# Attention output kept transposed and divided by GpSimd, against transposed and divided per head on TensorE and VectorE

## The chip, the cores and the metric

One core of one Trainium2 chip runs the whole program. The metric is the device time of one execution in microseconds (us). TensorE (PE in the rows) multiplies matrices, VectorE (DVE) and ScalarE (ACT) work on its results, GpSimd (POOL) works in SBUF and issues its own transfers, and SyncE (SP) only issues transfers.

## The reference, cut to what matters

Four images of 32 x 32 tokens with 192 channels go through attention with 12 heads of 16 channels and a relative position bias, then through a feed-forward layer that sends each token to one of 8 experts.

```python
x = x + proj(attention(layernorm(x)))      # 4 images x 12 heads, n = 1024 tokens each
  # attn = softmax(q * scale @ k.T + bias)   (n x n);  out = attn @ v   (n x 16)
  # out of the 12 heads side by side, @ proj_w.T + proj_b
t = layernorm(x)
gate = t @ Wg.T + bg                        # the best of 8 experts for each token
out = t_x + p(expert) * W3 (silu(W1 t) * (W2 t))
```

The softmax is computed as exponentials of scores less a row maximum; the weighted values are divided by the sum of the exponentials at the end. This division is what the change moves.

## The kernel before, in words

**Stages.** `project` normalizes the tokens and makes queries, keys, values and the bias tables. `attention` runs over 48 steps, a head of an image each (image fastest: step n is head n // 4 of image n % 4). `gate` multiplies with the output projection, adds the residual, normalizes again and computes the gate. `route` sorts tokens by expert, `experts` computes them. Each stage is a block: all engines meet at its end.

**A step of attention.** Each engine follows a written order; steps 4 to 43 are a hardware loop of four on TensorE, ScalarE, VectorE and SyncE, while GpSimd's program is written out. TensorE goes through four rounds (u = 0 to 3). A round is two score tiles (L796, 128 keys x 512 queries each, in a ring of three PSUM banks), two raw score tiles (L762, 128 queries x 1024 keys, in two PSUM buffers) of a head one or two steps ahead, two score tiles more, and the weighted values (L808) of the round before. VectorE takes the maximum of each raw tile (L921): eight a head. ScalarE takes the exponential of each score tile (L904): sixteen a head. Raw tile t has to wait for the maximum of tile t - 2, since there are two buffers.

**The maxima's way.** When VectorE has a head's eight maxima (after round 0 of the step before it), GpSimd copies them (L658), TensorE transposes them at the end of round 1 (L787), ScalarE copies the result (L886) and SyncE stores it into the extra row of that head's query tile (L621).

**SyncE's order.** Step n: eight loads of products for head n + 3 (`load_products`, L526 to L530) once the scores of step n - 1 are through, the store of the maxima for n + 1, and eight loads of positions for n + 3 (`load_positions`, L541 and L542). TensorE waits for all sixteen of head n + 2 at round 1 of step n (L845).

**The output of a head, the part that is changed.** `out_ps` holds, for each quarter of the image's queries, 32 rows: 16 channels, the sum of the exponentials in row 16, zeros. ScalarE copies it to `out_t` after the fourth exponential of the next step (`copy_out`, L892). TensorE turns it at the end of round 2 (`turn_out`, L814: 16 weight loads and 16 small float32 passes into a bank of the score ring, position 13 of 18). VectorE inverts the sums and multiplies (`normalize`, L923: L931 and L936) into `att_sb`, token by token. The ring bank is free for scores again only when `att_done` has come (L779).

**GpSimd in attention.** Besides the values (L666) and the maxima's copies it splits the experts' weights: in steps 4 to 39 a load of 234 KB a step (L697, L701) and the split of one (L681 to L688), and every five steps a load (L713), a split (L720, L721) and a store (L722) of W3, 384 KB each.

**The start of `gate`.** SyncE loads W3 (L1250). For each half image s TensorE turns `att_sb` (`turn_attention`, L1081), ScalarE copies it (`copy_attention`, L1146), and TensorE projects (`project_out`, L1092); VectorE adds the residual and takes statistics (`residual`, L1200, L1204). GpSimd clears `slot_rows` (L1045) and normalizes (L1056).

## Time and profile before

| | us |
|---|---|
| median of 3 runs (lowest, highest) | 873.83 (872.3, 876.49) |
| the profiled execution, its own time | 873.62 |
| its span, first to last instruction | 871.6 |
| first to last start of L819 (`turn_out`) in the span | 155.8 to 640.8 |
| mean granted TensorE clock | 0.952 |

The profile is of one execution, and all positions are microseconds from the start of its span. A row of the timeline has a start, a length, the engine, the line, the operation and the tiles, a count where rows were merged, and in brackets the idle time before it with what ended it. PEld is TensorE's loading of weights, which runs beside its multiplying; a name with q at its end (SPq, POOLq) is the engine's queue issuing a transfer.

### The profile page before, as it was taken

The numbers are of one execution on the slowest core, as the hardware profiler recorded it, in microseconds if no ns is written. First come the engines' busy times: TensorE is split into PE (matmuls) and PEld (weight loads), VectorE is DVE, ScalarE is ACT, GpSimd is POOL, SyncE is SP. The second block draws the span as 40 slices with busy tenths as digits, with TensorE's granted clock in tenths as the row PEclk, the third lists the DMA queues.
The fourth block names the chain that finished last, engine by engine and source line by source line (L and its number), as shares of the span: only waits on it lengthen the run. The fifth ranks groups of instructions, "written<-read, shape, count | busy, mean of one in ns | idle before, by whom it ended". The sixth has DMA issues, their size and how long they took to land. (4 is left out here: it accounts for less than half of the span.)

```text
span 871.6 us, 32001 instructions
## 1 busy us (share of the span) xinstructions
PE 781.6 (90%) x11826; PEld 477.4 (55%) x11826; DVE 712.9 (82%) x983; ACT 628.8 (72%) x1142; POOL 288.7 (33%) x437
## 2 busy tenths in 40 slices
PE   4999939999999999999999999999989617999994
PEld 1678803444444444444444444444468516999994
DVE  5976768999999999998999999989537665888883
ACT  3676615888888888888888888888955514667662
POOL 5630000013343423302234233421114403677762
PEclk9999958999999999999999999999999757999998
DMA  6346963444554455445444555554044403555560
GB/s 178 81 132 188 366 227 106 107 121 139 141 145 140 133 129 137 118 119 143 111 139 134 139 143 135 150 140 111 4 164 131 166 25 74 121 138 122 137 108 13
DMA packets 89866, 114.56 MB, mean 131 GB/s; under 512 B 40267, under 2 KB 56809, under 8 KB 88274
## 3 DMA queue, kind: packets, MB, share of 16 engines
q1 hardware_dynamic: 79248, 80.35, 33.9%
q0 software_dynamic: 9248, 26.51, 11.4%
q10 hardware_dynamic: 1314, 6.95, 2.1%
q8 instruction: 36, 0.59, 0.3%
q14 instruction: 20, 0.16, 0.1%
HBM read 77.58 MB, written 33.19 MB: 127 GB/s over the span
## 5 line engine op out<-in xcount | busy, mean ns | idle before, releaser
L921 DVE TENSOR_REDUCE neg_max<-max_ps 128x1 f16<-128x1024 f32 x384 | 452.3, 1221 | 38.3 <-PE max_ps L762 30.4
L904 ACT ACTIVATE probs<-ring_ps 128x512 f32<-128x512 f32 x768 | 413.6, 596 | 67.1 <-PE ring_ps L796 58.1
L796 PE MATMUL ring_ps<-q_side,k_side 113*32 113x512 f16 x3072 | 239.0, 383 | 8.3 <-DMA q_side<-rel_split 4.8
L808 PE MATMUL out_ps<-probs,values 128*32 128x256 f32 x3072 | 199.5, 379 | 0.2 <-ACT probs L904 0.2
L762 PE MATMUL max_ps<-k_side,q_side 48*128 48x256 f16 x1536 | 136.6, 278 | 15.8 <-ACT ident L879 9.2
L808 PEld LDWEIGHTS out_ps<-probs,values 128*32 128x32 f32 x3072 | 92.3, 110 | 70.4 <-ACT probs L904 0.7
L658 POOL COPY max_copies<-neg_max 128x32 f16<-128x32 f16 x48 | 10.1, 210 | 347.4 <-DVE neg_max L921 347.4
L796 PEld LDWEIGHTS ring_ps<-q_side,k_side 113*32 113x32 f16 x3072 | 73.2, 94 | 92.6 <-ACT probs L904 39.2
L762 PEld LDWEIGHTS max_ps<-k_side,q_side 48*128 48x128 f16 x1536 | 48.9, 95 | 119.8 <-issue 70.7
L1487 PE MATMUL hid_ps<-slot_t,w_top 128*118 128x128 f16 x312 | 68.9, 221 | 0.8 <-DVE w_top L1577 0.8
L1491 PE MATMUL hid_ps<-slot_t,w_tail 128*118 128x128 f16 x312 | 68.8, 220 | 0.0
L1490 PE MATMUL hid_ps<-slot_t,w_tail 128*118 128x128 f16 x312 | 68.8, 220 | 0.0
L1489 PE MATMUL hid_ps<-slot_t,w_top 128*118 128x128 f16 x312 | 68.8, 220 | 0.0
L1488 PE MATMUL hid_ps<-slot_t,w_top 128*118 128x128 f16 x312 | 68.7, 220 | 0.0
L1451 POOL DMA_INDIRECT slot_rows<-token_rows,slot_token x39 | 45.6, 1169 | 39.3 <-issue 39.3
L1466 POOL DMA_INDIRECT out<-y,slot_token x39 | 44.3, 1135 | 36.9 <-DVE y L1572 21.0
L1541 ACT ACTIVATE w_tail<-expert_weights 128x944 f16 x39 | 38.5, 990 | 12.6 <-PEq L1295 8.3
L1599 DVE TENSOR_TENSOR hidden<-hid_ps,silu 118x512 f32<-118x512 f32 x39 | 27.0, 692 | 24.1 <-PE hid_ps L1491 18.9
L1554 ACT ACTIVATE silu<-hid_ps 118x512 f32<-118x512 f32 x39 | 23.3, 597 | 28.6 <-PE hid_ps L1491 28.6
L1487 PEld LDWEIGHTS hid_ps<-slot_t,w_top 128*118 128x118 f16 x312 | 41.9, 134 | 1.2 <-DVE w_top L1577 1.0
L1488 PEld LDWEIGHTS hid_ps<-slot_t,w_top 128*118 128x118 f16 x312 | 41.9, 134 | 0.0
L1491 PEld LDWEIGHTS hid_ps<-slot_t,w_tail 128*118 128x118 f16 x312 | 41.9, 134 | 0.0
(235 smaller groups left out, 1326.0 us busy)
## 6 DMA issues: line engine op xcount, KB each, us to landing
q_side<-rel_split SPq DMA_DIRECT2D x384, 64.0 KB, 2.3
q_side<-qk_split SPq DMA_DIRECT2D x192, 64.0 KB, 2.5
rel_split<-expert_weights ACTq DMA_DIRECT2D x6, 1024.0 KB, 4.9
rel_split<-expert_weights SPq DMA_DIRECT2D x6, 1024.0 KB, 6.0
q_side<-qk_split SPq DMA_DIRECT2D x48, 128.0 KB, 2.7
k_side<-qk_split SPq DMA_DIRECT2D x144, 32.0 KB, 1.8
token_rows<-tn_parts SPq DMA_DIRECT2D x8, 512.0 KB, 3.4
expert_weights<-in_w_t POOLq DMA_DIRECT2D x32, 117.2 KB, 3.0
```

Source lines behind the costliest of these rows:

```text
L762: last = nc.tensor.matmul(max_ps[t % 2][:, keys], q_side[j][at:at + HIGH, quarter, t * P:(t + 1) * P], k_side[j][at:at + HIGH, keys], star ...
L796: last = nc.tensor.matmul(ring_ps[turn_of(k) % BANKS][at:at + COLS, :], k_side[slot(s)][:, tile * P + at:tile * P + at + COLS], queries, s ...
L808: last = nc.tensor.matmul(out_ps[quarter * 2 * HD:(quarter + 1) * 2 * HD, :], values[j][:, tile, :], probs[:, u % 2 * GROUP + 2 * i + quar ...
L904: nc.scalar.activation(probs[:, u % 2 * GROUP + i, :], ring_ps[turn_of(k) % BANKS][:], ACT.Exp).then_inc(exp_done, 1)
L921: nc.vector.tensor_reduce(neg_max[:, j % 2, t:t + 1], max_ps[t % 2][:], AX, ALU.max, negate=True).then_inc(tile_max, 1)
L1451: pool.indirect_dma_start(rows[:, j, :], None, g.token_rows, bass.IndirectOffsetOnAxis(ap=g.slot_token[:, n:n + 1], axis=0), bounds_check= ...
L1466: pool.indirect_dma_start(g.out_rows, bass.IndirectOffsetOnAxis(ap=g.slot_token[:, n:n + 1], axis=0), y[:, j, :], None, bounds_check=last_ ...
L1487: nc.tensor.matmul(out, w_top[:, j, h, 0, some], hi_top, start=True, stop=False, skip_group_check=True)
L1488: nc.tensor.matmul(out, w_top[:, j, h, 0, some], lo_top, start=False, stop=False, skip_group_check=True)
L1489: nc.tensor.matmul(out, w_top[:, j, h, 1, some], hi_top, start=False, stop=False, skip_group_check=True)
L1490: nc.tensor.matmul(out, w_tail[:, j, h, some], hi_tail, start=False, stop=False, skip_group_check=True)
L1491: last = nc.tensor.matmul(out, w_tail[:, j, h, some], lo_tail, start=False, stop=True, skip_group_check=True)
```

## The change

`turn_out`, `normalize`, `turn_attention` and `copy_attention` go. The output stays with channels in partitions, in `g.att_t` (two halves of 96 channels x 4096 tokens, and a row of ones below the second for the projection's bias).

- The value tiles are set to one instead of zero beyond their 16 channels, so that rows 16 to 31 of each quarter all hold the sum.
- `copy_out` writes one of four buffers of `out_t`, and waits for the product four heads back.
- GpSimd moves the sums of a head (4 rows x 256) within SBUF to 128 partitions x 8 (`load_sums`). VectorE inverts them one head later (`invert_sums`, at round 1). GpSimd stores the inverses, 4 KB, to DRAM (`store_inverse`) and loads them back with every sum repeated over 32 rows, 128 KB (`spread_inverse`). Four heads after its scores GpSimd multiplies (`scale_output`, 128 x 256 float32) and stores 128 KB to DRAM (`store_output`).
- SyncE's loop is written out, as steps 28 to 31 and 47 have loads of `att_t` in them (`load_outputs`). The last head of each image does not go through DRAM: `place_output` in `gate`.
- `gate` begins with the end of this chain for steps 44 to 47; SyncE loads W3 only at its third turn.
- Buffers of other stages are laid into the new tiles (`xn`, `xt`, the W3 parts, `y`); memory for `v_sb`'s column of ones and its setting fall away.

The diff, cut:

```diff
+def load_sums(queue, g, n):
+    queue.wait_ge(g.out_copied, n + 1)
...
+    queue.dma_start(g.sums[:, n % 2, :], g.out_t[HD::2 * HD, n % OUTS, :]).then_inc(g.sums_loaded[n % 2], 16)
+def invert_sums(nc, dve, g, slot, head, reused):
...
+    nc.vector.reciprocal(g.inverse[:, slot % 2, :], g.sums[:, slot % 2, :]).then_inc(g.inverted, 1)
+def store_inverse(queue, g, n):
+    queue.wait_ge(g.inverted, n + 1)
...
+    queue.dma_start(g.inverse_dram[n % 2].rearrange("q n -> (q n)").rearrange("(p c) -> p c", p=P), g.inverse[:, n % 2, :]).then_inc(g.inverse_stored[n % 2], 16)
+def spread_inverse(queue, g, n):
...
+    every_row = g.inverse_dram[n % 2].rearrange("q (o n) -> q o n", o=1).broadcast_to([4, 2 * HD, N // 4])
+    queue.dma_start(g.spread[:, n % 2, :], every_row).then_inc(g.inverse_spread[n % 2], 16)
+def scale_output(nc, pool, g, n):
...
+    nc.gpsimd.tensor_tensor(g.scaled[:, n % 2, :], g.out_t[:, n % OUTS, :], g.spread[:, n % 2, :], ALU.mult).then_inc(g.output_scaled, 1)
+def store_output(queue, g, n):
...
+    by_quarter = g.att_dram[head, :, image * N:(image + 1) * N].rearrange("c (q n) -> q c n", q=4)
+    queue.dma_start(by_quarter, g.scaled[:, n % 2, :]).then_inc(g.placed[image], 16)
...
-            steps(sp, BH, SLOTS, step)
+            for n in range(BH):
+                step(Step(n, n // SLOTS, n % SLOTS, BH, True))
...
+                if s.before(4):
+                    scale_output(nc, pool, g, s.n - 4)
+                if s.before(1):
+                    load_sums(pool, g, s.n - 1)
+                if s.before(3):
+                    spread_inverse(pool, g, s.n - 3)
+                if s.before(4):
+                    store_output(pool, g, s.n - 4)
...
-                    if u == 2 and s.before(1):
-                        bank_free(s, TURNED_AT)
-                        turn_out(s.n - 1)
...
-                        normalize(s.n - 1, head(s, -1), slot(s, -1), s.before(2))
+                    if u == 1 and s.before(2):
+                        invert_sums(nc, dve, g, slot(s, -2), head(s, -2), s.before(4))
```

**Three places in the order.** GpSimd in step 28, before, from its copy of the maxima to the next values:

```order
L658 COPY max_copies<-neg_max 128x32 [waits tile_max,max_t_ready]
L713 DMA w_whole<-in_w_rows 128x768
L687 CAST expert_weights<-expert_weights 128x469 [waits top_loaded1]
L688 TENSOR_TENSOR expert_weights<-expert_weights 128x469 [waits weights_split]
L701 DMA expert_weights<-in_w_t 128x469 [waits weights_split]
L666 COPY values<-v_sb 128x8x17 [waits group_done]
```

and the same stretch now:

```order
L741 COPY max_copies<-neg_max 128x32 [waits tile_max,max_t_ready]
L590 TENSOR_TENSOR scaled<-out_t,spread 128x256 [waits placed2,inverse_spread0]
L547 DMA sums<-out_t 128x1x8 [waits inverted,out_copied]
L576 DMA spread<-inverse_dram 128x1x256 [waits output_scaled,inverse_stored1]
L599 DMA att_dram<-scaled 4x32x256 [waits output_scaled]
L805 DMA att_t<-in_w_rows 128x768
L778 CAST expert_weights<-expert_weights 128x469 [waits top_loaded0]
L779 TENSOR_TENSOR expert_weights<-expert_weights 128x469 [waits weights_split]
L792 DMA expert_weights<-in_w_t 128x469 [waits weights_split]
L566 DMA inverse_dram<-inverse 128x8 [waits inverse_spread0,inverted]
L749 COPY values<-v_sb 128x8x16 [waits group_done]
```

A product and three transfers stand ahead of the expert's load, and a fourth transfer behind it, with a wait for VectorE.

TensorE at the end of round 2, before (each x7 or x3 completes the row above it):

```order
L808 MATMUL out_ps<-probs,values 32x256 [waits exp_done]
L808 MATMUL out_ps<-probs,values 32x256 x7
L782 REGISTER_ALU
L819 MATMUL ring_ps<-ident_sb,out_t 32x68 [waits out_copied,exp_done]
L819 MATMUL ring_ps<-ident_sb,out_t 32x68 x7
L796 MATMUL ring_ps<-q_side,k_side 32x512 [waits exp_done]
```

and now:

```order
L907 MATMUL out_ps<-probs,values 32x256 [waits exp_done]
L907 MATMUL out_ps<-probs,values 32x256 x7
L881 REGISTER_ALU
L895 MATMUL ring_ps<-q_side,k_side 32x512 [waits exp_done]
L895 MATMUL ring_ps<-q_side,k_side 32x512 x3
```

The next round's scores follow the weighted values directly.

GpSimd at the start of `gate`, where before one clearing (L1045) stood ahead of the normalizing, now:

```order
L547 DMA sums<-out_t 128x1x8 [waits inverted,out_copied]
L590 TENSOR_TENSOR scaled<-out_t,spread 128x256 [waits placed2,inverse_spread0]
L576 DMA spread<-inverse_dram 128x1x256 [waits output_scaled,inverse_stored1]
L566 DMA inverse_dram<-inverse 128x8 [waits inverse_spread0,inverted]
L1122 MEMSET slot_rows 128x2688
L590 TENSOR_TENSOR scaled<-out_t,spread 128x256 [waits placed3,inverse_spread1,rows_zeroed]
L576 DMA spread<-inverse_dram 128x1x256 [waits output_scaled,inverse_stored0]
L566 DMA inverse_dram<-inverse 128x8 [waits inverse_spread1,inverted]
L590 TENSOR_TENSOR scaled<-out_t,spread 128x256 [waits last_placed0,inverse_spread0]
L576 DMA spread<-inverse_dram 128x1x256 [waits output_scaled,inverse_stored1]
L1138 TENSOR_SCALAR tn<-x_sb,rstd,shift 128x192 [waits shift2_done]
```

The last three heads' products and transfers now stand ahead of the first normalizing there, and the last head's product behind it.

## Rows read from the trace of the kernel before

**Rows 1.** Groups by line: count | busy us, mean ns | idle before, releaser.

```profile
L921 DVE TENSOR_REDUCE neg_max<-max_ps 128x1 f16<-128x1024 f32 x384 | 452.3, 1221 | 38.3 <-PE max_ps L762 30.4
...
L819 PE MATMUL ring_ps<-ident_sb,out_t 128*32 128x68 f32 x768 | 19.7, 222 | 0.6 <-ACT out_t L892 0.6
```

**Rows 2.** Timeline of one steady head, TensorE, VectorE and SyncE's queue.

```profile
415.52 0.22 PE L787 MATMUL ring_ps<-ident,max_copies 128*32 128x128 f16 x1
...
418.15 0.41 PE L819 MATMUL ring_ps<-ident_sb,out_t 128*32 128x68 f32 x16
...
418.39 0.60 PE L796 MATMUL ring_ps<-q_side,k_side 113*32 113x512 f16 x8
...
418.85 0.20 DVE L931 RECIPROCAL recip<-ring_ps 128x8 f32<-128x8 f32 x1
...
419.39 4.78 DVE L921 TENSOR_REDUCE neg_max<-max_ps 128x1 f16<-128x1024 f32 x4
...
419.53 0.20 PEld L796 LDWEIGHTS ring_ps<-q_side,k_side 113*32 113x32 f16 x8 [0.27 <-DVE att_sb L936]
...
420.44 0.37 SPq L542 DMA_DIRECT2D q_side<-rel_split  x1
...
420.84 0.61 PE L796 MATMUL ring_ps<-q_side,k_side 113*32 113x512 f16 x8
...
421.79 0.11 PEld L762 LDWEIGHTS max_ps<-k_side,q_side 48*128 48x128 f16 x4 [0.31 <-DVE neg_max L921]
...
423.43 0.60 PE L796 MATMUL ring_ps<-q_side,k_side 113*32 113x512 f16 x8
...
424.40 2.36 DVE L921 TENSOR_REDUCE neg_max<-max_ps 128x1 f16<-128x1024 f32 x2 [0.23 <-PE max_ps L762]
...
425.86 0.22 PE L787 MATMUL ring_ps<-ident,max_copies 128*32 128x128 f16 x1
```

**Rows 3.** Waits, 160 to 630 us: total us, times, longest.

```profile
PEld ring_ps L796 <- DVE att_sb L936: 14.0, 45, 0.6
...
PE ring_ps L796 <- DMA q_side<-rel_split: 4.4, 6, 1.4
```

**Rows 4.** One line's transfers (L542), issue to landing.

```profile
DMA to landing us min/median/max: 2.0/2.2/4.5
```

**Rows 5.** Stretches of 1 us: busy time by engine, PEclk, DMA share, GB/s.

```profile
378.00:379.00 1.00, 0.97 (x20) 0.23 (x9) 0.93 (x2) 0.79 (x3) 0.00 (x0) 1.00 0.47 131
...
439.00:440.00 1.00, 1.00 (x32) 0.48 (x20) 0.83 (x3) 0.55 (x3) 0.00 (x0) 1.00 0.88 207
```

**Rows 6.** Timeline of GpSimd: a store of W3.

```profile
405.15 0.57 POOL L722 DMA_DIRECT2D w_split<-w_parts  x1 [0.30 <-POOL w_parts L721]
```

**Rows 7.** Timeline of TensorE, the longest stall of the loop.

```profile
413.13 0.62 PE L796 MATMUL ring_ps<-q_side,k_side 113*32 113x512 f16 x8 [1.41 <-DMA q_side<-rel_split]
```

**Rows 8.** Groups by line, GpSimd.

```profile
L1451 POOL DMA_INDIRECT slot_rows<-token_rows,slot_token x39 | 45.6, 1169 | 39.3 <-issue 39.3
...
L688 POOL TENSOR_TENSOR expert_weights<-expert_weights 128x469 f16<-128x469 f32 x16 | 17.3, 1079 | 1.4
...
L666 POOL COPY values<-v_sb 128x136 f32<-128x136 f32 x48 | 15.0, 312 | 0.9
...
L721 POOL TENSOR_TENSOR w_parts<-w_whole,w_parts 128x768 f16<-128x768 f32 x8 | 13.2, 1645 | 0.7
```

**Rows 9.** Timeline, end of attention and start of the gate stage.

```profile
637.09 0.71 PE L796 MATMUL ring_ps<-q_side,k_side 113*32 113x512 f16 x8 [0.23 <-DVE att_sb L936]
...
640.01 0.38 ACT L892 ACTIVATE out_t<-out_ps 128x256 f32<-128x256 f32 x1 [1.19 <-PE out_ps L808]
...
641.85 2.34 POOL L1045 MEMSET slot_rows<- 128x2688 f32 x1 [16.99 <-POOLq L566]
...
645.81 0.85 PE L1092 MATMUL proj_ps<-proj_w_top,at_top 96*128 96x192 f32 x2
...
670.46 0.56 DVE L1200 TENSOR_TENSOR x_sb<-proj_ps,x_sb 128x384 f32<-128x384 f32 x1 [2.59 <-PE proj_ps L1092]
```

More of the change, by code:

```diff
@@ new lines, in place_output, with load_outputs @@
+def place_output(sp, g, n):
+    sp.wait_ge(g.output_scaled, n + 1)
+    image = n % B
+    for q in range(4):
+        queries = slice(image * N + q * N // 4, image * N + (q + 1) * N // 4)
+        sp.dma_start(g.att_t[C - HD:C, 1, queries], g.scaled[2 * HD * q:2 * HD * q + HD, n % 2, :]).then_inc(g.last_placed[image], 16)
+HALF_HEADS = HEADS // 2
+def load_outputs(sp, g, image, c):
+    heads = range(HALF_HEADS) if c == 0 else range(HALF_HEADS, HEADS - 1)
+    tokens = slice(image * N, (image + 1) * N)
+    sp.wait_ge(g.placed[image], 16 * heads.stop)
+    sp.dma_start(g.att_t[0:HD * len(heads), c, tokens], g.att_dram[heads.start:heads.stop, 0:HD, tokens]).then_inc(g.outputs_loaded[image], 16)
@@ L545 @@
+OUTS = 4
 K_LO = HD + 2 * HS
@@ L641, in step @@
                     load_positions(sp, g, head(s, 3), slot(s, 3))
-            steps(sp, BH, SLOTS, step)
+                if TOPS_LOADED <= s.n < TOPS_LOADED + B:
+                    load_outputs(sp, g, s.n - TOPS_LOADED, 0)
+                if s.n == BH - 1:
+                    for image in range(B):
+                        load_outputs(sp, g, image, 1)
+            for n in range(BH):
+                step(Step(n, n // SLOTS, n % SLOTS, BH, True))
         @block.gpsimd
@@ L777, in bank_free @@
                         return pe.wait_ge(max_copied, s.n - back + 2)
-                    if at == TURNED_AT and s.before(1 + back):
-                        return pe.wait_ge(att_done, s.n - back)
-                    if at not in (MAX_AT, TURNED_AT):
-                        k = at - (at > MAX_AT) - (at > TURNED_AT)
+                    if at not in (MAX_AT, UNUSED_AT):
+                        k = at - (at > MAX_AT)
                         return pe.wait_ge(exp_done, 2 * KT * (s.n - back) + k + 1)
@@ L995, in gate @@
         psum = lambda name, shape: ctx.enter_context(nc.psum_tensor(name, shape, F32))
-        at_ps = [psum(f"at_ps{c}", [C, HALF]) for c in range(2)]
         tt_ps = [ctx.enter_context(nc.psum_tensor(f"tt_{part}_ps", [P, 2 * HALF], F16)) for part in ("hi", "lo")]
@@ L1020, in _ @@
         def _(sp):
-            load_experts(sp, g, experts_loaded)
+            last = BH - 1
+            for n in range(BH - B, last):
+                place_output(sp, g, n)
             def store_residual(s):
@@ L1035, in _ @@
                     store_residual(b)
+                if b == 2:
+                    place_output(sp, g, last)
+                    load_experts(sp, g, experts_loaded)
                 if b >= LAG + 1:
@@ L1069, in _ @@
                     normalize(b - 2)
+                if b == 2:
+                    scale_output(nc, pool, g, last)
         @block.tensor
@@ L1073, in _ @@
             pe.wait_ge(g.gate_loaded, CONSTS)
-            def turn_attention(s):
-                if s:
-                    pe.wait_ge(at_ready, 2 * s)
-                for c in range(2):
-                    for i in range(TPS):
-                        last = nc.tensor.transpose(at_ps[c][:, i * P:(i + 1) * P], g.att_sb[:, TPS * s + i, c * C:(c + 1) * C], g.ident[:])
-                    last.then_inc(at_ps_ready, 1)
             def project_out(s):
-                pe.wait_ge(at_ready, 2 * s + 2)
+                if s % 2 == 0:
+                    pe.wait_ge(g.outputs_loaded[s // 2], 32)
+                    pe.wait_ge(g.last_placed[s // 2], 64)
                 for i in range(TPS):
@@ L1681, in build @@
         g.x_sb = sb("x_sb", [P, TT, D])
-        g.att_sb = sb("att_sb", [P, TT, D])
-        g.gates = sb("gates_sb", [P, TT, EXPERTS])
-        g.tile_expert = sb("tile_expert", [P, FFN_TILES], I32)
-        g.slot_token = sb("slot_token", [P, FFN_TILES], U32)
+        g.att_t = sb("att_t", [P, 2, T])
+        g.out_t = sb("out_t", [P, OUTS, N // 4])
+        g.spread, g.scaled = (sb(name, [P, 2, N // 4]) for name in ("spread", "scaled"))
+        g.sums, g.inverse = (sb(name, [P, 2, N // P]) for name in ("sums", "inverse"))
+        sem = lambda name: ctx.enter_context(nc.semaphore(name))
+        g.out_copied, g.inverted, g.output_scaled = sem("out_copied"), sem("inverted"), sem("output_scaled")
+        g.ones_row_set = sem("ones_row_set")
+        g.sums_loaded, g.inverse_stored, g.inverse_spread = (
+            [sem(f"{name}{j}") for j in range(2)] for name in ("sums_loaded", "inverse_stored", "inverse_spread"))
+        g.placed, g.last_placed, g.outputs_loaded = ([sem(f"{name}{j}") for j in range(B)] for name in ("placed", "last_placed", "outputs_loaded"))
         g.ident16 = sb("ident16", [P, P], F16)
```

151 lines of the change are left out of this document (77 added, 74 removed).

## The prediction

> **What bounds the kernel now.** I read the groups by line first: VectorE's maxima alone are 452.3 us [rows 1], most of the 485 us that attention takes. Then the timeline of one steady head. A head takes 425.86 - 415.52 = 10.34 us between two transposes of the maxima [rows 2], and the reader should see two engines that both have hardly a gap in it. VectorE: eight maxima at 4.78 / 4 = 1.195 us are 9.56, and from the start of the inverse to the next maximum 419.39 - 418.85 = 0.54 go to the division; 0.23 are idle, waiting for TensorE [rows 2]. TensorE: the rounds that begin at 418.39, 420.84 and 423.43 take 2.45, 2.59 and 2.43, and 418.39 - 418.15 = 0.24 is the turning of the output [rows 2]. The round of 2.59 is the one whose raw tile waits 0.31 for a maximum [rows 2]; VectorE is late there since it has just divided. So the two hold each other through the two raw buffers: TensorE's own round is about 2.43, VectorE's two maxima are 2.39, and what either has on top shows in part.
>
> A third chain is nearly as tight. The last load of positions is issued at 420.44 and lands after 2.2 (median) [rows 2, 4], at 422.64; the scores that need it, with the raw tiles of the same head, start at 423.43 [rows 2]. It is 0.8 us early. Where a store of W3 and an expert's load are in the way [rows 6] it is late, and TensorE stalls, 1.41 at most [rows 7], six times and 4.4 us in all from 160 to 630 us [rows 3].
>
> **The change, part by part.** The sum is made against the profiled execution: a span of 871.6, 873.6 with what lies around it, which is the median of the runs within 0.3 us.
>
> *TensorE's turning.* 768 small passes go (19.7 us busy, four beside each other [rows 1]), and on the path 0.24 a head. The wait of scores for the ring bank (14.0 us in 45 places [rows 3]) goes with it; those are waits of weight loads beside running work, so I cost them at nothing, and what covers them is the multiplying; without that cover they are worth 0.3 a head.
>
> *VectorE's division.* 0.54 becomes one inverse of 128 x 8, for which I take the old one's 0.20 [rows 2]. Its two waits (sums loaded, old inverses stored) have been ready for most of a head, as both are issued a head or more earlier; behind it on VectorE queue the maxima. The old 0.54 showed as 2.59 - 2.44 = 0.15 on the path, so the remaining 0.20 shows as 0.06. Gain 0.09. Bounds: nothing, and the whole 0.54 - 0.20 = 0.34 if VectorE's 0.23 of waiting also closes up.
>
> A steady head gains 0.24 + 0.09 = 0.33 and takes 10.0; there are 44 such steps: 14.5 us. ScalarE, which keeps all its work, has pauses in this loop and doesn't get to be the bound: sixteen exponentials, two copies.
>
> *GpSimd's new work.* A product of 128 x 256: the two rows of 469 and 768 elements give (1645 - 1079) / 299 = 1.89 ns an element and hence 0.68 us [rows 8]. Four issues at 0.57 [rows 6] are 2.3. A head with a W3 split has 0.31 + 0.21 for the copies, 3.0 new, 0.83 + 1.65 + 0.57 for W3, 1.66 + 0.56 for an expert: 8.8 of 10.0 [rows 6, 8] (the lengths not in the rows are estimated from the two rows' slopes). It is hidden by GpSimd's waiting for maxima; if an issue costs what an indirect one does, 1.17 [rows 8], such a head has 11.2 and the maxima's copy is 1.2 late in 8 heads, up to 10 us.
>
> *Transfers.* 264 KB more move a head, 256 of it in two pieces of 128 KB. And three issues and the product, 2.4 us, now stand ahead of each load of an expert and each store of W3, which move by as much toward SyncE's last positions. With a head 0.33 shorter, these are 0.47 early. How late can they get? In the worst stall, 384 KB of W3 and 234 KB of an expert made them 1.41 + 0.8 = 2.2 late [rows 6, 7], 3.6 ns per KB; 256 KB are 0.9 at that rate, a stall of 0.43 a head, 19 us. From the other side: 234 KB alone, which most heads already have, lift the engines' share from 0.47 to 0.88 for a microsecond [rows 5] and stall none of them; the new pieces are issued about when SyncE begins its positions, and there are four microseconds to catch up; a store of W3 now comes when most positions have landed, and the 4.4 may shrink. I take 3 us, nearer to the quiet heads, because the share is 0.47 in an ordinary stretch, and keep -4 to +19.
>
> The rows show late loads only for large pieces spread over all engines. The Trainium skill (page "DMA: Bandwidth & Descriptors", section "Why a DMA increments its semaphore by 16 and not by 1") says that a transfer is split over as many of the 16 engines as divide the slowest dimension of both its sides; `store_output`, with 4 quarters as its slowest, would go over 4. No trace here shows it. By that rule the full rate of rows 5 (131 / 0.47 = 279 GB/s) leaves 70 for it, an estimate of 1.9 us on these four instead of 0.5 on all, and the transfer term would be nearer to its upper end.
>
> *SyncE written out.* The same issues, without the loop's address arithmetic; nothing, as the chain is waited on at its end.
>
> *The end of attention.* The last two heads lose the turning and a bank wait that nothing covers there, 0.24 + 0.23 each [rows 2, 9]. After the last copy, at 640.01 + 0.38, the turning and the division go and the stage ends at about 640.7 instead of 641.85 [rows 9]. Together 2.1.
>
> *Gate.* The first projection started at 645.81 [rows 9]. Now, from 640.7: an issue 0.57, the product 0.68, four issues on SyncE at 0.37 [rows 2] and 2.2 to land: 645.6. No gain, and TensorE comes to it idle. After that its turns of 8 transposes, and ScalarE's copies, are gone; VectorE's wait of 2.59 for a projection [rows 9] closes. GpSimd's chain of the last heads stands ahead of its normalizing, for which VectorE's own work leaves room. I take 2.5 gained, between 0 and 4.
>
> Sum: -14.5 - 2.1 - 2.5 + 3 = -16.1, 857.5 us.
>
> **Rivals.**
>
> *The whole gain* (0.12). VectorE's pauses close too, 0.5 a head: 22 + 2.1 + 2.5, and the stalls' 4.4 halve: about 845. For it: VectorE's load falls to 9.76. Against: TensorE's four rounds and the transpose alone are 9.8.
>
> *Half eaten by transfers* (0.15). A stall of 0.25 in each steady head: 11 us, 865.5.
>
> *Slower: positions late in every head* (0.12). The expert's load moved onto the last positions adds 234 x 3.6 ns = 0.83 to the 0.9: 1.7 late, 1.2 of stall in the 32 heads that have such a load, 0.43 in 12: 45 us in all, 899. But the stall comes after the maxima that release GpSimd, so GpSimd's transfers slide away from the positions again; with half of it given back 877. The middle is 888. It decides from a lateness of 0.47 + 0.43 = 0.9, where the stall eats what the head gains.
>
> *No change* (0.08). The change doesn't do what it says: the division comes back as waiting, on GpSimd (the 10 us above) or in `gate`, where the projection of the second half of the images waits for GpSimd's chain. About 871.
>
> **How the numbers follow.** The forecast has 0.53. Faster by over 0.5%, about what a measurement of this kernel can tell from no change, is the forecast, the whole gain and half eaten: 0.80. Same 0.08, slower 0.12. The range reaches from the whole gain to the no-change case: 846 to 874.
>
> **What would show it.** Right: transposes of the maxima 10.0 us apart, no round of 2.59, VectorE's line of maxima at a higher share of attention, waits for `q_side` of some 5 to 8 us in all, the first projection near 645.6 less what attention gained. Wrong: a wait of score rounds on `q_side` in most heads (transfers); waits of the transpose for `max_copies` (GpSimd); the period still 10.3 with no wait on transfers (the division wasn't on the path).

## The result, and the profile after

The changed kernel takes 945.12 us (median of 4 runs, 939.97 to 956.23) against 873.07 before: a ratio of 1.0806, with a 95% interval of 1.0757 to 1.0856. The ratio leaves out the execution of 956.23 us, which fell as a whole into a slower state, and it puts the changed kernel at 943 us, the number that all comparisons below use. It is 70 us slower, where 857.5 was forecast and 874 was the upper end. The rows below are from a second profiled execution (f4_after_again), which took 937.34 us; its span is 935.5, and its mean granted clock is 0.923 (0.952 before).

First the page's busy time by engine: no engine is near its span, TensorE has 84% of it.

```profile
PE 786.5 (84%) x10994; PEld 457.5 (49%) x10994; DVE 702.0 (75%) x934; ACT 624.6 (67%) x1126; POOL 445.6 (48%) x673
```

The loop of attention is where the time is. The transposes of the maxima, one a head, mark its steps:

```profile
L886 PE MATMUL ring_ps<-ident,max_copies x48: 219/219/314, 126.5 to 682.4; 128*32 128x128 f16 x48
```

The same row before:

```profile
L787 PE MATMUL ring_ps<-ident,max_copies x48: 219/219/289, 126.9 to 624.5; 128*32 128x128 f16 x48
```

So 47 steps take 555.9 us instead of 497.6: 58.3 of the 63.9 by which the spans differ. The other 6 come after the last transpose (253.1 us to the end, 247.1 before).

The waits in that stretch, 160 to 680 us, which answer to [rows 3]:

```profile
DVE neg_max L1006 <- PE max_ps L863: 98.6, 121, 4.7
...
PE ring_ps L895 <- DMA q_side<-rel_split: 48.6, 28, 3.8
POOL spread L576 <- DMA inverse_dram<-inverse: 36.4, 18, 6.2
```

The wait of scores for the ring bank (14.0 us) is gone, as the change promises. But TensorE's waits for positions rose from 4.4 us in 6 places to 48.6 in 28. VectorE's waits for TensorE rose with them, from 18.2 us before: it gets its raw tiles late.

```profile
DVE neg_max L921 <- PE max_ps L762: 18.2, 52, 1.8
```

The third row of the waits after is new: GpSimd waits for its own store of inverses.

The transfers in the same stretch say why (queue and size, median us from issue to landing; before, positions landed after 2.2, as [rows 4] has it for one line):

```profile
q_side<-rel_split SPq DMA_DIRECT2D x344, 64.0 KB, 3.1
...
spread<-inverse_dram POOLq DMA_DIRECT2D x43, 128.0 KB, 3.8
att_dram<-scaled POOLq DMA_DIRECT2D x42, 128.0 KB, 4.5
...
inverse_dram<-inverse POOLq DMA_DIRECT2D x44, 4.0 KB, 4.7
```

One bad head, by its timeline:

```profile
349.60 0.72 POOL L590 TENSOR_TENSOR scaled<-out_t,spread 128x256 f32<-128x256 f32 x1
...
350.27 0.74 POOL L547 DMA_DIRECT2D sums<-out_t  x1
...
351.01 0.70 POOL L576 DMA_DIRECT2D spread<-inverse_dram  x1
...
351.70 0.70 POOL L599 DMA_DIRECT2D att_dram<-scaled  x1
...
352.04 0.58 SPq L537 DMA_DIRECT2D q_side<-rel_split  x1
...
352.39 0.60 POOL L805 DMA_DIRECT2D att_t<-in_w_rows  x1
...
355.03 1.08 POOL L788 DMA_DIRECT2D expert_weights<-in_w_t  x2 [0.29 <-POOL expert_weights L773]
355.76 0.30 SPq L538 DMA_DIRECT2D q_side<-rel_split  x1
...
362.47 1.05 PE L895 MATMUL ring_ps<-q_side,k_side 113*32 113x512 f16 x8 [3.83 <-DMA q_side<-rel_split]
```

Spread and store are issued just ahead of SyncE's eight loads of positions (352.04 to 355.76), a W3 load and an expert's load into the middle of them. The last positions land 6.7 us after their issue, and TensorE stands for 3.83. The share of the 16 transfer engines in stretches of this head (the last two columns are DMA share and GB/s, PEclk ahead of them):

```profile
351.00:353.00 2.00, 2.00 (x41) 0.96 (x37) 1.75 (x3) 1.92 (x5) 2.00 (x5) 1.00 0.22 25
353.00:355.00 2.00, 1.93 (x36) 0.71 (x32) 1.97 (x3) 1.69 (x4) 1.65 (x2) 1.00 0.84 181
355.00:357.00 2.00, 2.00 (x40) 0.91 (x32) 1.71 (x2) 1.63 (x4) 1.93 (x4) 1.00 0.87 253
357.00:359.00 2.00, 1.64 (x30) 0.59 (x24) 1.95 (x2) 1.82 (x5) 0.01 (x1) 1.00 1.03 220
359.00:361.00 2.00, 0.00 (x0) 0.00 (x0) 0.41 (x1) 0.18 (x1) 1.40 (x3) 1.00 1.07 187
361.00:363.00 2.00, 0.53 (x8) 0.23 (x8) 0.00 (x0) 0.00 (x0) 0.19 (x1) 0.75 0.55 98
```

From 351 to 353, while the sums' load moves and spread and store begin, four fifths of the engines' time is idle; from 357 to 361 all are busy, at 187 to 220 GB/s, though 253 was reached from 355 to 357. TensorE has been idle since 358.6 when the granted clock falls to 0.50 (1.2 GHz) at 362, and it is back at 1.00 only by 370 (0.50 in each stretch from 362 to 368, 0.79 from 368 to 370; the 0.75 of the last row is a mean over the fall). The eight matmuls behind the stall take 1.05 instead of 0.61. So a stall costs more than its own length: this step takes 16.04 us, 5.85 more than an undisturbed one, of which 3.83 are the stall. Not all heads are like this. One undisturbed head still shows what the change gains, 410.51 - 400.33 = 10.18 us against 10.34 in [rows 2]:

```profile
400.33 0.22 PE L886 MATMUL ring_ps<-ident,max_copies 128*32 128x128 f16 x1
...
401.18 0.19 DVE L557 RECIPROCAL inverse<-sums 128x8 f32<-128x8 f32 x1
401.32 0.11 PEld L863 LDWEIGHTS max_ps<-k_side,q_side 48*128 48x128 f16 x4 [0.27 <-DVE neg_max L1006]
...
402.96 0.61 PE L895 MATMUL ring_ps<-q_side,k_side 113*32 113x512 f16 x8
...
403.79 0.11 PEld L863 LDWEIGHTS max_ps<-k_side,q_side 48*128 48x128 f16 x4 [0.18 <-DVE neg_max L1006]
...
405.42 0.68 PE L895 MATMUL ring_ps<-q_side,k_side 113*32 113x512 f16 x8
...
406.34 0.11 PEld L863 LDWEIGHTS max_ps<-k_side,q_side 48*128 48x128 f16 x4 [0.20 <-DVE neg_max L1006]
...
407.98 0.61 PE L895 MATMUL ring_ps<-q_side,k_side 113*32 113x512 f16 x8
...
408.88 0.12 PEld L863 LDWEIGHTS max_ps<-k_side,q_side 48*128 48x128 f16 x4 [0.25 <-DVE neg_max L1006]
...
410.51 0.22 PE L886 MATMUL ring_ps<-ident,max_copies 128*32 128x128 f16 x1
```

A measure for the rest of this text: the **excess**, the sum over steps 2 to 45 of the time between two transposes, less 44 undisturbed steps (10.33 us in kernels with the old output, 10.19 with the new). It was 6.7 us before and is 71.4 now, in 36 of the 44 steps more than 0.2. So 64.7 us more are lost in disturbed heads, 44 x 0.14 = 6.2 are gained in all, and 6 are lost after attention: 64.5, near the 63.9 of the spans.

### The profile page after: what moved, and what is told of

The parts are those of the page before. It is cut to its first block and busy times, and to the rows that moved or that the text cites. A ratio compares the mean times of both kernels' runs of the same rounds, so it can differ in the third digit from the quotient of the medians.

```text
span 954.4 us, 29489 instructions
## 1 busy us (share of the span) xinstructions
PE 800.5 (84%) x10994; PEld 461.8 (48%) x10994; DVE 702.2 (74%) x934; ACT 624.9 (65%) x1126; POOL 444.6 (47%) x673
## 5 line engine op out<-in xcount | busy, mean ns | idle before, releaser
L895 PE MATMUL ring_ps<-q_side,k_side 113*32 113x512 f16 x3072 | 257.4, 406 | 63.6 <-DMA q_side<-rel_split 53.6
L907 PE MATMUL out_ps<-probs,values 128*32 128x256 f32 x3072 | 210.7, 396 | 0.2 <-ACT probs L989 0.2
L863 PE MATMUL max_ps<-k_side,q_side 48*128 48x256 f16 x1536 | 141.3, 290 | 16.7 <-ACT ident L963 9.2
L895 PEld LDWEIGHTS ring_ps<-q_side,k_side 113*32 113x32 f16 x3072 | 70.0, 96 | 175.4 <-issue 84.4
L907 PEld LDWEIGHTS out_ps<-probs,values 128*32 128x32 f32 x3072 | 95.7, 114 | 83.6 <-issue 13.2
L863 PEld LDWEIGHTS max_ps<-k_side,q_side 48*128 48x128 f16 x1536 | 52.7, 98 | 121.7 <-issue 77.9
L1531 POOL DMA_INDIRECT out<-att_t,slot_token x39 | 44.3, 1136 | 35.3 <-DVE att_t L1637 20.2
L576 POOL DMA_DIRECT2D spread<-inverse_dram x48 | 33.4, 696 | 45.8 <-DMA inverse_dram<-inverse 40.2
```

What stands on the lines that cost most here:

```text
L863: last = nc.tensor.matmul(max_ps[t % 2][:, keys], q_side[j][at:at + HIGH, quarter, t * P:(t + 1) * P], k_side[j][at:at + HIGH, keys], star ...
L895: last = nc.tensor.matmul(ring_ps[turn_of(k) % BANKS][at:at + COLS, :], k_side[slot(s)][:, tile * P + at:tile * P + at + COLS], queries, s ...
L907: last = nc.tensor.matmul(out_ps[quarter * 2 * HD:(quarter + 1) * 2 * HD, :], values[j][:, tile, :], probs[:, u % 2 * GROUP + 2 * i + quar ...
L1531: pool.indirect_dma_start(g.out_rows, bass.IndirectOffsetOnAxis(ap=g.slot_token[:, n:n + 1], axis=0), y[:, j, :], None, bounds_check=last_ ...
```

## The experiments

Three explanations stood at the start. **Few engines**: spread and store each go over four of the 16 transfer engines, and the positions, which go over all, wait for those. **Bytes**: 256 KB more a head are too much, however they are spread. **Order**: GpSimd's four new operations push the experts' loads and the W3 stores onto the last positions. SyncE's loop, now written out, was a fourth. Times are medians; ratios are to the kernel before on the same chip.

### Taking the two large transfers away, or spreading them

**e1_small**: both cut to 4 KB, issued at the same places. It leaves out the scaling and the heads' output, and its loads of outputs read other rows of the same size.

```diff
-    queue.dma_start(g.spread[:, n % 2, :], every_row).then_inc(g.inverse_spread[n % 2], 16)
+    queue.dma_start(g.spread[0:4, n % 2, :], every_row[:, 0, :]).then_inc(g.inverse_spread[n % 2], 16)
...
-    queue.dma_start(by_quarter, g.scaled[:, n % 2, :]).then_inc(g.placed[image], 16)
+    queue.dma_start(by_quarter[:, 0, :], g.scaled[0:4, n % 2, :]).then_inc(g.placed[image], 16)
...
```

> The changed kernel with its two large transfers of a head, the spread of the inverses and the store of the product, cut from 128 KB to 4 KB each; GpSimd still issues both at the same places and does the product. It leaves out the scaling by the right inverses and the output of the heads (loads_outputs reads other rows of the same size). If the two transfers themselves delay the positions (by their bytes or by the few engines that carry them), the waits for positions fall from some 50 us to under 10 and the time to about 862 us. If GpSimd's delay of the experts' loads and of the W3 stores does it, the waits stay and it takes over 930. If SyncE's written-out loop does it, also over 930.

893.45 us, 1.0235 (1.0148 to 1.0323). The two transfers' size is the larger part of the loss, 50 us, but not all of it: the waits for positions are still 21.1 us, the excess 29.2. Neither theory had a number between.

**e2_wide_store**: the stored product gets 128 rows in memory, and is loaded back a head at a time.

```diff
-    by_quarter = g.att_dram[head, :, image * N:(image + 1) * N].rearrange("c (q n) -> q c n", q=4)
-    queue.dma_start(by_quarter, g.scaled[:, n % 2, :]).then_inc(g.placed[image], 16)
+    queue.dma_start(g.att_dram[head, image], g.scaled[:, n % 2, :]).then_inc(g.placed[image], 16)
...
```

> Only the layout of the stored product differs: 128 rows of 1 KB, which all 16 transfer engines can share, instead of 4 x 32 rows, which four carried in the trace. The same 128 KB at the same place, and the loads of it one head at a time (16 rows). If a transfer on four engines is what holds up the positions, half of the loss goes: about 900 us, and the packets of 4 KB stand on 16 engines. If the bytes do it, 940 to 950 as before; if GpSimd's order does it, the same.

931.76 us, 1.0674 (1.056 to 1.0788): some 12 us gained of 70, less than the half that was expected, and the interval touches that of the changed kernel.

**e3_wide_both**: in addition the spread in four transfers of 32 rows.

```diff
-    queue.dma_start(g.spread[:, n % 2, :], every_row).then_inc(g.inverse_spread[n % 2], 16)
+    for q in range(4):
+        queue.dma_start(g.spread[2 * HD * q:2 * HD * (q + 1), n % 2, :], every_row[q]).then_inc(g.inverse_spread[n % 2], 16)
...
```

> Both large transfers over all engines: the store as in the run with the wide store, the spread as four transfers of 32 rows, which costs GpSimd three more issues a head (about 2 us, hidden as far as it waits for maxima). Few engines as the cause: nearly the whole loss goes, 865 to 880 us. Bytes as the cause: 940 or more. GpSimd's order as the cause: worse than the changed kernel, about 960, since the experts' loads come 2 us later still.

901.57 us, 1.0329 (1.0232 to 1.0425), excess 31.6: as low as with 4 KB (29.2), although all 256 KB still move and GpSimd issues three transfers more. So few engines cost 943 - 902 = 41 us, with the narrow loads of outputs counted in; bytes some 8 (902 against 893), which two runs each with overlapping intervals hardly show, and bytes alone fall as the explanation. It is not the 865 to 880 expected; a second cause is left.

### The second cause: order, or written-out code

**e4_late**: product, spread and store behind the experts' loads and W3's store.

```diff
+                if n >= 4:
+                    scale_output(nc, pool, g, n - 4)
...
                 if n >= 2:
                     store_inverse(pool, g, n - 2)
+                if n >= 3:
+                    spread_inverse(pool, g, n - 3)
+                if n >= 4:
+                    store_output(pool, g, n - 4)
```

(the same calls go from ahead of the weights; `load_sums` stays there)

> Transfers as in the changed kernel, but GpSimd does the product, the spread and the store behind the experts' loads and the W3 store, so that these stand where they stood before but for one issue. If the delay of the experts' loads is the cause, the time falls to 870 to 880 us. If the two narrow transfers are the cause, they now fall onto the loads of the products, which are wanted later than the positions: part of the loss goes, about 900. If the bytes of a head as such are the cause, 940 or more.

967.02 us, 1.1078 (1.0935 to 1.1222): worse by 24, with an excess of 96.1. That a later place is a cheaper one was wrong. Why it is a dearer one is not shown. The four-engine transfers now meet the loads of products, and the positions come behind these on SyncE's queue; but from 160 to 600 us the queries among these loads land after 3.3 us, as in the changed kernel, and the positions after 3.3 for 3.1, while the spread takes 5.6 for 3.7 and the store 6.3 for 4.5.

**e5_small_late** (the 4 KB transfers in this late order) and **e8_wide_late** (the wide ones in it):

> The run with the two large transfers cut to 4 KB (893 us, still 21 us of waits for positions), now with GpSimd's product, spread and store behind the experts' loads and W3's store. It leaves out what that run left out. If those remaining waits come from the experts' loads and W3 stores standing later on GpSimd, they fall to some 5 us and the time to 870 to 875. If they come from SyncE's written-out loop or from the four small transfers themselves, it stays at 885 to 895.

> Both large transfers over all engines, as in the run with both wide (902 us), and behind the experts' loads on GpSimd. If the order is the second cause beside the few engines, 880 to 885 us. If the 256 KB then collide with the loads of the products, which stand ahead of the next positions on SyncE's queue, no gain: 900 to 910.

892.65 us, 1.0243 (1.0184 to 1.0302), and 905.0, 1.0382 (1.032 to 1.0445). Neither differs from the same transfers at the place of the change (893 and 902): giving the experts' loads their old place back by moving the new work behind them gains nothing that shows.

**e6_unrolled** and **e7_delay** put one suspect each into the kernel before:

```diff
-            steps(sp, BH, SLOTS, step)
+            for n in range(BH):
+                step(Step(n, n // SLOTS, n % SLOTS, BH, True))
```

```diff
                     repeat_max(s.n + 1, slot(s, 1), s.before(1))
+                    if s.before(4):
+                        for i in range(3):
+                            nc.gpsimd.memset(delay[:], 0.0).then_inc(delayed, 1)
+                            pool.wait_ge(delayed, 3 * (s.n - 4) + i + 1)
```

> The kernel before, with only SyncE's loop of attention written out. If the fetching of SyncE's instructions makes its loads late, it is slower by 10 us or more, with waits for positions of 15 to 20 us; by the theory that GpSimd's order (and the transfers) do it, no change: 874 within 3 us.

> The kernel before, with 3 us of clearing of an unused tile put on GpSimd after each copy of the maxima from step 4 on, so that the experts' loads and W3's stores come 3 us later and nothing else is added. If that delay makes the positions late, 10 to 20 us slower, 885 to 893, with 15 to 20 us of waits for positions. If it doesn't, 874 within 3 us.

Written-out code: 874.13 us, 1.0028 (0.9993 to 1.0063), excess 7.6: nothing that this can tell from no change. The delay of 3 us: 878.67, 1.0085 (1.0047 to 1.0122). Its profiled execution, with 883.72 one of the longer ones, has an excess of 21.0 and waits for positions of 12.0 us in 10 places, longest 2.8. So GpSimd's delay is a cause, of some 7 us in the kernel before, less than the 10 to 20 that were expected of it.

**e9_none**: as the late run with 4 KB, without any of the four transfers of a head (sums, inverses, spread, store).

```diff
-    queue.dma_start(g.sums[:, n % 2, :], g.out_t[HD::2 * HD, n % OUTS, :]).then_inc(g.sums_loaded[n % 2], 16)
+    queue.sem_inc(g.sums_loaded[n % 2], 16)
...
```

> The run with small transfers and GpSimd's late order (893 us), with all four transfers of a head left out: sums, inverses, spread and store; the product and VectorE's inverse stay and work on ones. It leaves out the scaling and the heads' output. The waits for positions that are left in that run are 25 us above an undisturbed step's time, of which some 7 lie where SyncE loads the outputs back (steps 28 to 34). If the four transfers, small as they are, make the rest, the excess falls to 10 to 13 us and the time to 875 to 880. If the loads of outputs and the experts' loads make it, it stays at 888 to 893.

877.09 us, 1.0065 (1.0036 to 1.0093). So the four small transfers, with their issues and the waits for their landing, cost some 15 us by the ratios. And a kernel that keeps the division off TensorE and moves nothing for it but the loads of outputs is still not faster than the one before. Its excess is 16.3, of it 5.5 in steps 28 to 32, where SyncE loads the outputs of the first six heads; before, these steps had 0.5.

### Earlier instead of later

**e10_early** and **e11_early_wide** are complete kernels: product, spread and store stand ahead of the copy of the maxima, as soon as six (four) of the eight maxima are there, the store is wide, and the outputs are loaded back one head at a time over all engines; the second has the wide spread, too.

```diff
+                if s.before(3):
+                    if s.after(1):
+                        pool.wait_ge(tile_max, KT * (s.n + 2) - 2)
+                    if s.before(4):
+                        scale_output(nc, pool, g, s.n - 4)
+                    spread_inverse(pool, g, s.n - 3)
+                    if s.before(4):
+                        store_output(pool, g, s.n - 4)
                 if s.after(1):
                     repeat_max(s.n + 1, slot(s, 1), s.before(1))
```

> Complete kernel. Store wide (128 rows), spread still over four engines; GpSimd does product, spread and store ahead of its copy of the maxima, as soon as the sixth of the eight maxima is there, so that both transfers run while SyncE's queue has little left and the experts' loads stand again where they stood before but for one issue. Outputs are loaded back one head at a time, two in a step, over all engines. If it is the meeting with the positions that costs, and not the bytes: 875 to 885 us, against 932 with the wide store at the old place. If the time of issue does not matter: 925 to 935.

> As the early run, with the spread as four transfers over all engines, begun when the fourth maximum is there. By the theory of few engines and of the time of issue: 868 to 878 us, unless GpSimd becomes full in the steps with a split of W3 and gives back some 10. If only the number of engines matters, as with both wide at the old place: 900.

906.79 us, 1.0434 (1.0398 to 1.047), and 911.99, 1.0473 (1.0429 to 1.0516): both far from the 875 to 885 and 868 to 878 that were expected. With the spread over four engines the earlier place is worth some 21 us by the ratios, against the run with the wide store alone; some 5 us of that lie in steps 28 to 32, where e10 also loads the outputs in smaller groups. With the wide spread e11_early_wide is 12 us slower, by the ratios, than e3_wide_both: the waits for positions stay (21.0 us, 20.5 there), and a new wait comes on top. Both stand in the waits of e11_early_wide, 130 to 660 us:

```profile
POOL spread L577 <- DMA inverse_dram<-inverse: 96.0, 39, 4.0
...
PE ring_ps L912 <- DMA q_side<-rel_split: 21.0, 26, 2.2
...
PE ring_ps L903 <- POOL max_copies L756: 15.8, 8, 4.6
```

GpSimd waits in 39 heads for its own 4 KB store of inverses to land, and the copy of the maxima now stands behind that wait: TensorE's transpose waits for it in eight heads. e10_early has the same two waits, 45.7 us in 23 places and 8.1 in 6.

### The disputed cost by itself

In e2 and e3 other things changed with the number of engines. These four put stores that nobody reads into the kernel before, behind the copy of the maxima: **f1_narrow** and **f2_wide** one of 128 KB a head, **f5_two_narrow** and **f6_two_wide** two, with 2 us of clearing ahead of them.

```diff
+                    if s.before(4):
+                        pool.wait_ge(scratched, 16 * (s.n - 4))
+                        pool.dma_start(scratch.rearrange("c (q n) -> q c n", q=4), g.x_sb[:].rearrange("p t d -> p (t d)")[:, 0:QN]).then_inc(scratched, 16)
```

(wide: the destination is `scratch` with 128 rows)

> The kernel before with one more store a head, 128 KB that nothing needs, from GpSimd behind its copy of the maxima, in the access pattern of the changed kernel's store (4 x 32 rows). By the theory of few engines: 20 to 30 us slower, 892 to 902, with the waits for positions 20 to 30 us. By the theory that only bytes count: within 5 us of the run with the wide store.

> The same additional store, the same 128 KB from the same place, but to 128 rows of 1 KB. By the theory of few engines: under 5 us slower than before, 872 to 877. By the theory that bytes count: as slow as the run with four engines.

> The kernel before with two additional stores of 128 KB a head over four engines each and some 2 us of clearing of an unused tile ahead of them, so that the experts' loads come 3.4 us later, as in the changed kernel. By the theory of a slack that the first lateness uses up: 40 to 65 us slower, 912 to 937. If the single costs only add up: 890 to 898. Were the cause elsewhere in the changed kernel, also under 898.

> The same, with both stores over sixteen engines. By the theory of few engines: what the delay alone cost (7.4 us) and little more, 878 to 885. If the bytes count once two of them meet: 895 or more.

| added to the kernel before | time | ratio (95%) | excess |
|---|---|---|---|
| one store over four engines | 880.11 | 1.010 (1.0071 to 1.013) | 12.5 |
| one store over sixteen | 872.35 | 0.9989 (0.9962 to 1.0016) | 6.6 |
| two over four, and the delay | 941.65 | 1.0796 (1.0735 to 1.0857) | 80.7 |
| two over sixteen, and the delay | 887.56 | 1.0188 (1.0133 to 1.0244) | 21.0 |

One store over sixteen engines costs nothing that could be measured, over four it costs 7.6 us: less than the 20 to 30 expected. Two over four with the delay cost 71 us, as much as the whole change, where the single costs sum to 7.6 + 7.6 + 7.4 = 23; 40 to 65 was expected for the theory that a first lateness uses up a slack. The same two over sixteen cost 17, a little above the 878 to 885 expected: some 10 more than the delay alone. So two transfers over four engines, with GpSimd's delay, are enough for a loss of this size in a kernel that has nothing else of the change, and 942 - 888 = 54 us of it go when only the stores' destination is another. Their landing times, 160 to 600 us, first the run with two narrow stores, then the one with two wide:

```profile
q_side<-rel_split SPq DMA_DIRECT2D x289, 64.0 KB, 3.0
scratch<-x_sb POOLq DMA_DIRECT2D x68, 128.0 KB, 4.4
```

```profile
q_side<-rel_split SPq DMA_DIRECT2D x322, 64.0 KB, 2.4
scratch<-x_sb POOLq DMA_DIRECT2D x77, 128.0 KB, 2.1
```

And how much of the 16 engines GpSimd's queue keeps busy in the first microsecond in which the stores move in a quiet head (packets, MB, share): narrow from 407.5 to 408.5, then wide from 384.2 to 385.2. The row ahead of each is of all queues.

```profile
DMA packets 80, 0.07 MB, mean 71 GB/s; under 512 B 64, under 2 KB 64, under 8 KB 80
...
q0 software_dynamic: 56, 0.07, 23.8%
```

```profile
DMA packets 126, 0.24 MB, mean 240 GB/s; under 512 B 64, under 2 KB 64, under 8 KB 126
...
q0 software_dynamic: 67, 0.21, 64.3%
```

23.8% are 3.8 engines. The same store lands 2.3 us later on four engines than on sixteen, and GpSimd's queue moves a third of the bytes in that microsecond. The size of the pieces is no rival: but for packets under 512 B the bytes go in 16 packets here and 62 there, of some 4 KB each.

**f3_weights_early** turns the finding on the kernel before: the experts' loads and W3's loads and stores come a step later, but early in it, ahead of the copy of the maxima, at the sixth of eight.

```diff
+                if due:
+                    pool.wait_ge(tile_max, KT * (s.n + 2) - 2)
+                    for transfer in due:
+                        transfer()
+                    due.clear()
                 if s.after(1):
                     repeat_max(s.n + 1, slot(s, 1), s.before(1))
...
-                    load_top(n - TOPS_FROM)
+                    due.append(lambda n=n: load_top(n - TOPS_FROM))
```

> The kernel before, complete, with the experts' loads and W3's loads and stores issued one step later but early in it, ahead of the copy of the maxima, when the sixth of eight maxima is there. If their meeting with the positions is what makes these late (6.5 us above the undisturbed steps in the kernel before), the time falls by 3 to 6 us, to about 867. If the time of issue does not matter, no change.

866.97 us, 0.9934 (0.9906 to 0.9963): 5.6 us faster than before, the only kernel here that beats it. The excess falls from 6.7 to 1.8, the longest wait for positions (160 to 630 us) from 1.4 to 0.6. The time of issue moves the positions in both directions.

**f4_after_again** is the changed kernel itself, whose rows stand above.

> The changed kernel again, for a trace of an undisturbed execution: 940 to 950 us, some 80 us of waits and their consequences above undisturbed steps of 10.19 us.

942.77 us, 1.0798 (1.0722 to 1.0873), excess 71.4.

## Why the prediction was wrong

**The step that failed: Transfers, "I take 3 us".** The third chain was named rightly, and its lateness decides. But its size was missed: the term stood at 3 us, between -4 and +19, and the disturbed heads of the profiled execution lose 64.7 us more than before. It was taken from the wrong rows. The 4 us a head "to catch up" and the 234 KB that stall nobody [rows 5] are transfers over all engines; the two new ones use four. The Trainium skill (page "DMA: Bandwidth & Descriptors", section "Why a DMA increments its semaphore by 16 and not by 1") gives the rule by which I weighed this, that the slowest dimension of both sides sets the number of engines. The trace agrees where it can be seen: 23.8% of 16 for a store whose slowest dimension is 4, and 32.2%, 5.2 engines, while hardly anything but the loads of five heads each moves (688 to 690 us of the changed kernel):

```profile
q1 hardware_dynamic: 57, 0.23, 32.2%
```

I applied it to `store_output` only, estimated 1.9 us for it, and said it would push the term to its upper end, which was 19. I missed that `spread_inverse` has the same shape, with the four quarters slowest, and that `load_outputs` has six or five. The measured 3.8 and 4.5 us to landing are about twice the landing on sixteen (2.1 in the run with two wide stores). The estimate for the one transfer, 1.4 us more than on all engines, was thus not far off (2.3 in f5 against f6); what the working lacked is the second such transfer and what that lateness does to the positions behind it.

**What else was in the term.** The estimate that the experts' loads come 2.4 us later left out a wait: GpSimd stands 36.4 us in 18 places for its stored inverses, and the weights stand behind it. And the two transfers of 4 KB stood in the sum only with their bytes. Four of that size cost some 15 us (e5 against e9), of which the part of these two is not known, and the 4 KB store of the inverses took 4.7 us to land between the large ones.

**Why so much together.** Single disturbances cost 7 to 8 us, three together 71. That fits the 0.8 us by which positions were early [rows 2]: what is within it is free, what is beyond stops TensorE in every head that has it. Excess over 0.2 us was in 11 of 44 steps with one narrow store, in 36 with two and the delay. The halved clock behind a long stall adds to it. That the slack is the whole reason is an argument; the runs show that the sum is no guide.

**The rival that came true** was the slower one, positions late in every head: they are late in most. The expert's load moved onto the last positions, which it named, is worth some 7 us by itself (e7); the four engines, which are the larger part, it didn't have. It had a chance of 0.12, and 888 for its time. Its price of 3.6 ns per KB came from transfers over all engines again; its upper figure, 899, is about what the kernel takes with both transfers wide (902). The range ended at 874, short of this rival; stretched to 899 it would still have missed.

**The head's gain** was forecast as 0.33 and is 0.16. The turning's 0.24 came: from one transpose to the next round is 418.15 - 415.52 = 2.63 before [rows 2] and 402.96 - 400.33 = 2.63 now, and the 0.24 behind it is gone. The division's 0.09 did not: the rounds that begin at 402.96, 405.42 and 407.98 take 2.46, 2.56 and 2.53, against 2.45, 2.59 and 2.43 before [rows 2], so 0.08 more. A raw tile waits for a maximum in each of the four rounds now, for 0.18 to 0.27. The prediction explained the round of 2.59 by the one such wait that it read, 0.31; but two other rounds of that head had one too, 0.27 and 0.39:

```profile
416.52 0.11 PEld L762 LDWEIGHTS max_ps<-k_side,q_side 48*128 48x128 f16 x4 [0.27 <-DVE neg_max L921]
...
418.93 0.33 PEld L762 LDWEIGHTS max_ps<-k_side,q_side 48*128 48x128 f16 x8 [0.39 <-DVE neg_max L921]
```

So a shorter division does not show as a shorter round. My reading, not tested, is that 4 x 2.43 on one side and 8 x 1.195 + 0.19 on the other alternate through two buffers, and neither runs at its own pace. So the prize was half of what I counted, 6 to 7 us in 44 heads.

**Right**: the bank waits went, and no gain beyond the turning's 0.24 shows for them; GpSimd's product took 0.72 (0.68 forecast) and its issues 0.56 to 0.74; SyncE's loop written out costs nothing that could be measured (e6).

**The end of attention and `gate`** were forecast to gain 4.6 us and lost 6. SyncE's and GpSimd's rows around the stage boundary show the chain:

```profile
683.49 14.94 SPq L621 DMA_DIRECT2D att_t<-att_dram  x4
...
702.35 6.77 SPq L609 DMA_DIRECT2D att_t<-scaled  x8
```

```profile
SPq L621 <- DMA att_dram<-scaled: 11.9, 2, 8.3
```

```profile
692.92 0.70 POOL L599 DMA_DIRECT2D att_dram<-scaled  x1
...
697.42 0.38 ACT L977 ACTIVATE out_t<-out_ps 128x256 f32<-128x256 f32 x1 [1.19 <-PE out_ps L907]
697.74 0.69 SPq L621 DMA_DIRECT2D att_t<-att_dram  x1
...
700.33 1.28 ACT L1212 ACT_TABLE_LOAD   x1 [2.53 <-PEq L646]
```

```profile
706.69 0.98 PE L1169 MATMUL proj_ps<-proj_w_top,att_t 96*128 96x192 f32 x2 [9.34 <-DMA att_t<-scaled]
...
720.38 1.96 POOL L1138 TENSOR_SCALAR tn<-x_sb,rstd,shift 128x192 f32<-128x192 f32 x4
```

The row of 14.94 is mostly waiting: in 660 to 730 us SyncE stands 11.9 us for stored products to land. The last of them is issued by GpSimd at 692.92 and lands 4.8 us later; the fourth load of outputs follows it and is issued by 698.43, after the last copy of an output (697.42 + 0.38). The first row of `gate` is at 700.33, 2.53 after that copy, where the prediction had it 0.3 after and the trace of before 1.47. Then the last heads' placing begins at 702.35, its four issues take 2.5 instead of 1.5, and TensorE stands for 9.34 in all. I had counted the chain from GpSimd's product onward (0.57, 0.68, four issues, 2.2) and left out the last store and the loads that stand ahead of it. GpSimd's first normalizing is at 720.38, 13.7 us behind the first projection; before, the first projection was at 645.81 [rows 9] and this normalizing started at 657.28:

```profile
657.28 3.88 POOL L1056 TENSOR_SCALAR tn<-x_sb,rstd,shift 128x192 f32<-128x192 f32 x8 [13.08 <-DVE shift L1279]
```

That is 11.5 us, so `gate` loses two more on its way.

**What stays open.** No view here tells one transfer engine from another, so that the positions wait on just the four engines of the narrow transfers is inferred from f5 and f6. Why the positions then move at only 187 to 220 GB/s with all engines busy, and how the 15 us of the small transfers divide between their time on the engines, their issues and the waits for them, was not tried.

## What to carry to other kernels

Before adding a transfer to a loop, look at the slowest dimension of both its sides: with 4 there, 128 KB took twice as long to land, and beside transfers that another engine waits for this cost 41 us of 943 here, while the same bytes over all engines cost some 8. Price a new transfer from a row of one with the same shape, not of the same size, and ask how much slack the nearest waiting chain has: beyond it, three disturbances together came to three times the sum of their single costs here. And a removed step on one of two engines that alternate through two buffers can give back less than its length; the time at which large loads are issued can give as much (5.6 us here) for nothing.

## What the runs showed of the hardware

- 128 KB from SBUF to memory, two such stores a head, took 4.4 us from issue to landing over four engines and 2.1 over sixteen (medians of f5_two_narrow and f6_two_wide), in otherwise equal kernels.
- A 4 KB store issued behind large transfers of the same queue took 4.7 us to land (median of 44, f4_after_again).
- With the share of the transfer engines at 1.03 and 1.07 the rate was 220 and 187 GB/s, lower than at 0.87 (253 GB/s, 355 to 357 us of the head above).
- TensorE stood for 3.83 us up to 362.47 in f4_after_again; from 362 to 368 the granted clock was 0.50 (1.2 GHz), though TensorE was busy again, and by 370 it was 1.00.
